# Attention with its query product ahead of the projections, a three-slot scan for the cell of a recurrence, and variance sums one tile later

## The reference, cut to what matters

```
q = (relu(x @ wq.T) + 1e-06) / softplus(scale);  k = (relu(x @ wk.T + pos) + 1e-06) / softplus(scale)
q, k = focus(q), focus(k)          # focus(t) = t^3 / |t^3| * |t|
z = 1 / (q . sum_j k_j + 1e-06)
y = (q @ (k^T v)) * z + depthwise_conv5x5(v)
out = y @ proj_w.T + proj_b
```

```
i = sigmoid(x U_i + h V_i + b_i); g = tanh(x U_c + h V_c + b_c); o = sigmoid(x U_o + h V_o + b_o)
cell = i * g + h * cell_before
h = o * tanh(cell)
```

## Time and profile before

| what | value |
|---|---|
| median of 3 runs | 1471.23 us (1469.86 to 1482.88) |
| profiled execution | 1470.42 us |
| its span, first to last instruction | 1468.5 us |
| instructions | 26362 |
| mean granted TensorE clock | 0.784 of full speed |

### The profile page before, as it was taken

The page is one execution under the profiler, slowest core; times in us unless marked ns, Lnnn a source line. Parts: engine busy times, 40 slices in busy tenths (PEclk is TensorE's granted clock), DMA queues, the critical chain, the costliest instruction groups (busy, mean ns, idle before and its releaser), DMA issues. The chain is left out here.

```text
span 1468.5 us, 26362 instructions
## 1 busy us (share of the span) xinstructions
PE 1125.3 (77%) x9003; PEld 648.5 (44%) x9003; DVE 888.7 (61%) x2711; ACT 505.0 (34%) x1330; POOL 245.2 (17%) x359
## 2 busy tenths in 40 slices
PE   6778877677998666666666656669947999999996
PEld 2356653343555344444444444437543333333332
DVE  6686736745776555555555555551264766666665
ACT  3443423452443222222222222234404334343432
POOL 3103102000000000000000000000001444454545
PEclk9899988878999855555555555569958999999999
DMA  7000000000000000000000000000005634554540
GB/s 270 0 2 2 1 2 0 1 0 1 1 0 1 1 1 0 0 0 0 0 0 0 0 0 0 0 1 0 0 0 108 136 95 112 103 111 105 105 111 7
DMA packets 23053, 46.90 MB, mean 32 GB/s; under 512 B 1616, under 2 KB 5840, under 8 KB 22608
## 3 DMA queue, kind: packets, MB, share of 16 engines
q1 hardware_dynamic: 22992, 46.10, 13.5%
HBM read 43.47 MB, written 2.62 MB: 31 GB/s over the span
## 5 line engine op out<-in xcount | busy, mean ns | idle before, releaser
L1587 PE MATMUL wide<-ls_h,ls_v 128*128 128x16 f16 x2304 | 104.8, 176 | 172.0 <-DVE ls_h L1680 172.0
L2017 PE MATMUL wide<-xpad,w 64*128 64x512 f32 x1024 | 228.7, 596 | 3.7 <-PEq L80 3.2
L2061 DVE TENSOR_TENSOR ex_hid<-wide,ex_gated 128x1024 f32<-128x1024 f32 x128 | 156.8, 1225 | 88.9 <-ACT ex_gated L2051 87.5
L2051 ACT ACTIVATE ex_gated<-wide 128x1024 f32<-128x1024 f32 x128 | 131.2, 1025 | 202.1 <-PE wide L2017 202.1
L1587 PEld LDWEIGHTS wide<-ls_h,ls_v 128*128 128x128 bf16 x2304 | 81.6, 106 | 241.0 <-DVE ls_h L1680 241.0
L1997 POOL TENSOR_TENSOR ex_acc<-ex_part,ex_acc 128x512 f32<-128x512 f32 x120 | 152.8, 1273 | 131.5 <-DVE ex_part L2072 117.0
L2017 PEld LDWEIGHTS wide<-xpad,w 64*128 64x128 f32 x1024 | 96.7, 187 | 134.5 <-issue 124.9
L1667 DVE SCALAR_TENSOR_TENSOR ls_ig<-ls_gates 128x16 f32<-128x16 f32 x256 | 53.0, 207 | 127.1 <-ACT ls_gates L1607 127.1
L1607 ACT ACTIVATE ls_gates<-wide 128x32 f32<-128x32 f32 x256 | 50.6, 198 | 229.0 <-PE wide L1592 229.0
L2029 PE MATMUL wide<-ex_hid,w 128*64 128x512 f32 x512 | 116.7, 598 | 0.0
L2072 DVE TENSOR_TENSOR ex_part<-wide,ex_d 128x1024 f32<-128x1024 f32 x64 | 78.4, 1225 | 30.1 <-PE wide L2029 27.3
(11 more groups left out here) (339 smaller groups left out, 1860.6 us busy)
## 6 DMA issues: line engine op xcount, KB each, us to landing
ex_d<-route SPq DMA_DIRECT2D x64, 512.0 KB, 7.8
par_attn<-in_attn SPq DMA_DIRECT2D x1, 2704.0 KB, 13.3
par_rest<-in_rest SPq DMA_DIRECT2D x1, 2139.0 KB, 17.8
L_xin<-in_x SPq DMA_DIRECT2D x8, 256.0 KB, 5.9
w<-in_w SPq DMA_DIRECT2D x1, 2048.0 KB, 22.2
out<-ex_acc SPq DMA_DIRECT2D x16, 128.0 KB, 4.4
w<-in_w SPq DMA_DIRECT2D x1, 512.0 KB, 23.0
route<-ro_dt SPq DMA_DIRECT2D x8, 64.0 KB, 1.7
```

The lines of the kernel that those rows point to most:

```text
L1587: pe.matmul(ig[:, g, :] if g < 2 else o, vp[part][:, g, :], h1[:], start=False, stop=False, skip_group_check=True)
L2017: mm = pe.matmul(pair_of_up(G, j)[:, h * TW:(h + 1) * TW], m.w12[r, (2 * e + w) * HID:(2 * e + w + 1) * HID], m.xn[r, t * TW:(t + 1) * TW] ...
L2051: act.activation(gated[:, n % 2, :], pair_of_up(n // GS, 2 * (n % GS))[:], ACT.Silu)\
L2061: dve.tensor_tensor(hid[:, n % (2 * GS), :], pair_of_up(n // GS, 2 * (n % GS) + 1)[:], gated[:, n % 2, :], ALU.mult).then_inc(s["hid_ready ...
```

## The change

In the attention the order of the full groups on TensorE becomes kv(G), attend(G), qkv(G+2), turn(G+1). On VectorE `divide(G)` stands ahead of `normalise(G+1)`, and the first sum is a step of its own. On ACT `turned(G)` stands ahead of `square_base(G+1)`. Mixed units are worked on with attend one unit behind, and k^T v of the mixed units alternates between wide[1] (banks 2 and 3) and wide[0] (banks 0 and 1). In the layer norm four centrings stand ahead of the first variance. In the recurrence the two instructions for the cell become one `tensor_tensor_scan` over 16 x 3 elements, in which the state is multiplied by `factors` and `addends` are added. The three slots of an image are (0, 1), (1, tanh of the input gate), (tanh g, hc), so the third result is g * (1 + t_i) + hc, which is twice the cell of before; the tanh behind it takes 0.5 times it. The gates, the cell and `hc` lie with a stride of three floats.

```diff
@@ attention, TensorE
-                pe.wait_ge(s["kvm_ready"], n)
+                pe.wait_ge(s["base_ready"], GROUPS if j % 2 else G + 1)
+                pe.wait_ge(s["kvm_ready"], n - 1 if n > FULL else n)
...
-            for G in range(GROUPS):
-                if G < FULL:
-                    kv(G)
+            for G in range(FULL):
+                if G % 4 == 0:
                     turn(G)
-                    if G + 2 < GROUPS:
-                        qkv(G + 2)
-                    attend(G)
+                kv(G)
+                attend(G)
+                qkv(G + 2)
+                if G % 4 == 3:
+                    finish_run(run_of(G))
                 else:
-                    for j in range(GU):
-                        kv_mixed(G, j)
-                        turn_mixed(G, j)
-                        attend_mixed(G, j)
-                if G in (3, 7, 9):
-                    finish_run(run_of(G))
+                    turn(G + 1)
+            for n in range(2 * GU + 1):
+                if n < 2 * GU:
+                    kv_mixed(FULL + n // GU, n % GU)
+                    turn_mixed(FULL + n // GU, n % GU)
+                if n:
+                    attend_mixed(FULL + (n - 1) // GU, (n - 1) % GU)
+            finish_run(2)
@@ attention, ScalarE
+            for G in range(FULL):
+                turned(G)
+                square_base(G + 1)
+                square_cube(G + 1)
+                root(G + 1)
+                values(G + 2)
+                if G + 1 == FULL:
                     masked(G + 1)
...
+            turned_mixed(FULL, 0)
+            square_base(FULL + 1)
+            turned_mixed(FULL, 1)
+            square_cube(FULL + 1)
+            turned_mixed(FULL, 2)
+            root(FULL + 1)
+            turned_mixed(FULL, 3)
+            masked(FULL + 1)
@@ attention, VectorE
+            for G in range(FULL):
+                base_of(G + 1)
+                mask(G)
+                cube_of(G + 1)
+                sum2(G + 1)
+                sum6(G + 1)
                 divide(G)
-                if G in (3, 7, 9):
+                normalise(G + 1)
+                if G % 4 == 3:
                     add_conv(run_of(G))
+            base_of(FULL + 1)
+            mask_mixed(FULL, 0)
+            cube_of(FULL + 1)
+            mask_mixed(FULL, 1)
+            sum2(FULL + 1)
+            mask_mixed(FULL, 2)
+            sum6(FULL + 1)
+            mask_mixed(FULL, 3)
+            normalise(FULL + 1)
+            divide(FULL)
+            for j in range(GU):
+                mask_mixed(FULL + 1, j)
+            divide(FULL + 1)
+            add_conv(2)
@@ layer norm, TensorE
-            for t in range(3):
+            for t in range(4):
                 centre(t)
-            for t in range(GT + 1):
+            for t in range(GT):
                 variance(t)
-                centre(t + 3)
-            variance(GT + 1)
+                centre(t + 4)
+            variance(GT)
             spread(0)
-            variance(GT + 2)
-            variance(GT + 3)
+            for t in range(GT + 1, TILES):
+                variance(t)
             spread(1)
@@ recurrence
+        N = HB * 3 + 2
+        flat = terms[:].rearrange("p z n -> p (z n)")
+        factors, addends = flat[:, 0:HB * 3], flat[:, N + 1:N + 1 + HB * 3]
+        cell, hc = cells[:, :, 2], addends.rearrange("p (b k) -> p b k", k=3)[:, :, 2]
+        two_gates = terms[:, :, 2:2 + HB * 3].rearrange("p z (b k) -> p z b k", k=3)[:, :, :, 0]
...
-                        act.activation(tc[:], cell[:], ACT.Tanh).then_inc(s["tc_ready"], 1)
+                        act.activation(tc[:], cell, ACT.Tanh, scale=0.5).then_inc(s["tc_ready"], 1)
...
-                        dve.scalar_tensor_tensor(ig[:], gates[:, 0, :], 1.0, gates[:, 1, :], ALU.add, ALU.mult)\
-                           .then_inc(s["ig_ready"], 1)
-                        dve.wait_ge(s["ig_ready"], t + 1)
                         dve.wait_ge(s["hc_ready"], t + 1)
-                        dve.scalar_tensor_tensor(cell[:], ig[:], 0.5, hc[:], ALU.mult, ALU.add)\
+                        dve.tensor_tensor_scan(cells[:].rearrange("p b k -> p (b k)"),
+                                               factors, addends, 0.0, ALU.mult, ALU.add)\
                            .then_inc(s["cell_ready"], 1)
```

79 lines of the change are left out of this document (26 added, 53 removed).

## The result

The changed kernel takes 1440.29 us (median of 4 runs, 1439.68 to 1441.81), the one before 1475.22 (median of 4, 1469.86 to 1482.88): a ratio of 0.9755 with a 95% interval of 0.9716 to 0.9795. The profiled execution took 1441.81 us, of which 1439.9 are its span; against the profiled one of before, 1470.42, that is 28.6 us less. By the ratio of all runs it is 36.0 us less (0.0245 x 1471.2). The two differ because the runs of before spread over 13 us and its profiled execution lies at their low end, while the profiled one of the changed kernel is the highest of its four.

The account below looks back on a forecast made before the run. No engine fills the span; the kernel is a row of stages, each with its own limit. Terms -33.0 + 4.0 + 0.2 - 8.8 - 0.2 = -37.8 us from 1470.4 give 1432.6, plus 0.8, rounded to 1434 us; range 1415 to 1448.

Parts of the forecast that it names:

- the likeliest case: Whole kernel: the forecast of 1434 us itself, own range 1426 to 1441 us, chance 0.62.
- The scan: Recurrence: two instructions become one scan at two cycles an element, 0.256 us, saving 0.129 us a step, 33.0 us.
- Both rate rivals: Recurrence scan: one element a cycle, 1422 us, chance 0.14; or as slow as the reciprocal, 1485 us, chance 0.04.
- Half of a bound of 7.9 us: Recurrence: the stride of three floats costs 0 to 7.9 us; half was taken, +4.0 us.
- PE's clock in the recurrence: Recurrence: clock taken to stay at 0.50; rival that it rises, 23 us less, 1411 us, chance 0.03.
- 2.5 + 3.5 = 6.0 us: Attention, mixed groups: masked copies start 2.5 us earlier; group 9, pipelined and nearer the low clock, gains 3.5 us.
- 2.8 us in all up to the mixed groups: Attention, full groups: gain from VectorE's filled hole and an earlier base(6), less later sums at run ends, 2.8 us.
- PE pays at the end of a run ... the sums start 0.6 us later: Attention, run ends: qkv waits for mask and attend, so the convolution sums start 0.6 us later against base.
- costs some 0.4 us in a group in which the clock is low: Attention, full groups: kv's cover is base alone, 1.13 against 0.76 us of matmul; low clock costs some 0.4 us.
- base(6) was to come 2.0 us earlier: Attention, group 6: with divide done before, base(6) is limited by qkv(6) and moves from 140.9 to 138.9.
- the attention gives nothing, since PE's clock falls at other places: Rival on the attention: kv and qkv then come late, no gain there, 1443 us, chance 0.11.
- The layer norms: Four layer norms: order changes, not the sum; 0 for three, 0.2 us gained before the recurrence, bounds ±0.3 each.

Follow-up runs that it names:

- the long scan: Changed kernel with the scan run over 96 elements instead of 48, the 48 more being zeros nobody reads: 1467.04 us, ratio 0.9943.
- the kernel with the strides alone: Kernel before with gates, cell and hc at a stride of three floats, without the scan: 1482.37 us, ratio 1.0053.
- the half alone: Kernel before with only the two mixed groups of the attention reordered, the eight full groups as before: 1464.10 us, ratio 0.9927.
- the kernel with the old full groups: Changed kernel with its eight full attention groups put back to the order of before on all three engines: 1440.31 us, ratio 0.9778.

## Why the prediction was right in sum, and where it was not

**The total.** 1434 us were forecast and 1440.29 measured, inside the range of 1415 to 1448 and, barely, inside the likeliest case's own of 1426 to 1441. As a ratio the forecast was 1434 / 1471.23 = 0.9747, and 0.9755 was measured. An agreement that close is luck. Between the two profiled executions 37.8 us less were forecast and 28.6 were measured; the attention gave 5.7 us less than forecast, the recurrence 2.2 less, and stages that nobody edited took 2.0 us more. The ratio came near all the same because the other executions of before were slower than its profiled one: the sum had 0.8 us for that, and the median of the four is 4.8 us above it.

**The scan, right.** 0.256 us forecast, 0.258 measured; 0.035 to ACT's start, 0.04 measured. The argument (the result of an element must be there before the next one starts, so two cycles each) chose the right rate, and the long scan shows the slope itself: 2.08 ns where 2.04 were taken. The runs show the rate and not its reason. The Trainium skill (DVE: opcode table, instruction layouts, handler registers and perf-mode slots, section 6, Datapath and trigger behaviour) says that the built-in scan runs at half throughput; the trace agrees, with 2.08 against 1.02 ns an element. Both rate rivals fall, 1.02 and 6.2 ns.

**The strides, undersized.** Half of a bound of 7.9 us was taken, 4.0; the two ACT instructions cost 23 ns a step, 5.9 us. Scan, starts and strides together: 1.740 us less the 0.105 gained is the 1.63 seen, 26.8 us for the recurrence against 33.0 - 4.0 = 29.0 forecast. Of the 2.2 us missing 1.9 are the strides. The measured 5.9 lie midway between the half that was taken and the whole bound; the kernel with the strides alone, in which VectorE writes a strided cell as well, shows 7.7. The Trainium skill (SBUF — State Buffer, section SBUF: two separate sides) says that each access that crosses to a new 16-byte line pays a penalty, without a figure for it; the trace agrees that there is one at a step of 12 bytes, 15 ns for 32 elements. What scaled wrong was the interpolation: the price was assumed to fall with the length of the step, from 64 bytes in the earlier trace rows down to 12, and per element it hardly does (0.64 ns there; 15 ns for 32 elements and 8 for 16 here, 0.5 ns each).

**PE's clock in the recurrence, right.** It stayed at the lower level; PE's fillers did not delay the nine matmuls, which waited for `h` as before (0.28 us in the step shown, 141.6 of 144.9 us over the stage).

**The mixed groups, right in kind and size.** 2.5 + 3.5 = 6.0 us were forecast for groups 8 and 9; the marks show 2.7 and 4.2 (15.12 to 12.45 and 16.55 to 12.33 us), and the half alone 7.1. Group 9 was nearer the full clock than assumed: only its first unit was slow after the idle time. The masked copies start 9.2 us after the first kv of group 8 instead of 11.86 and so come earlier within the group, as worked out; their place near 186 was missed (192.18), since they were to gain 2.8 us from the full groups and lost 3.9 there.

**The full groups, wrong sign.** This is the step that failed: "2.8 us in all up to the mixed groups". 3.95 us were lost instead, an error of 6.8 us: 3.0 at the two runs' ends, 1.7 behind the second run, 1.2 at base(6) and 1.0 in group 1. (For groups 5 to 7 the forecast has 0.75 us without its working; two periods at 0.42 would be 0.84.) Its parts:

- The period without the hole, 8.29 us, came as forecast wherever the clock was full, and `divide` of group 4 lost its wait of 4.46 us.
- "PE pays at the end of a run ... the sums start 0.6 us later" costed the swapped order only at the full clock. The run's end took 2.10 us more, not 0.6, with the clock at 0.54 in the projections; the transposes just behind it ran at 0.53. The kernel with that order put back at the run's end alone has 14.22 us there, at the clock 1.00, and is 7.4 us faster in the stage. That this order at this place is what starts the loss in the changed kernel is shown by it.
- "costs some 0.4 us in a group in which the clock is low": such a group was there (group 2), and it cost a `base` wait of 0.98 us on qkv, not a mask wait on kv. The thinner cover that mattered was that of the projections, which start behind `attend`; the prediction looked only at kv's.
- base(6) was to come 2.0 us earlier since qkv(6) would start at the same time. It starts 3.5 us later (136.40 against 132.92): 2.1 us come from the run's end and most of the rest from the slow transposes behind it, which stand ahead of the output projection and so of GpSimd's gather. It runs at a low clock too, and base(6) still waits 1.06 us for it. The same slow transposes stand behind the second run, and no term had the 1.7 us that the first mask of group 8 comes later for it.

The rival "the attention gives nothing, since PE's clock falls at other places" named this mechanism and gave it 0.11. It was right for half the stage. Its "against", that the hole is filled whatever the clock does, is true and not enough: the hole is filled and a wait for qkv opens in its stead.

**The layer norms, right.** Forecast -0.2 us in all, and alone they make no difference in the time. By the traces three of the four give 0.16, 0.43 and 0.16 us, one of them beyond its bound of 0.3.

**What no term had.** Code that nobody edited moved by +2.0 us in all between the two traces: whitening -2.1, slice attention +1.6, experts +2.5. The experts' first 70 us, before and after:

```profile
1111.00:1181.00 70.00, 66.23 (x302) 26.38 (x302) 43.09 (x36) 30.06 (x32) 24.19 (x19) 1.00 0.65 133
```
```profile
1080.00:1150.00 70.00, 66.14 (x289) 26.01 (x290) 41.65 (x34) 28.39 (x31) 22.27 (x18) 0.95 0.62 129
```

The clock fell in a piece of it in one and not in the other, and 13 matmuls fewer were done in the same time. Such stages also move between two executions of one program: in the changed kernel and in the same kernel once more the whitening takes 48.18 and 50.19 us, the slice attention 135.33 and 133.64, the sigmoid attention 65.88 and 67.90, where the attention takes 152.21 and 152.23.

**Still open.** Why the clock falls in exactly these stretches. Shown is that it follows holes of PE at the runs' ends (filling them, and making one of them shorter, removed it from there) and that one order can have it in different places in two kernels. What decides between the two is not shown; the start of the stage (72.1 against 74.1 us) went with it in the kernel with the old full groups, but the new attention took nearly the same from 72.4 and from 74.1.

## What to carry to other kernels

Before two instructions that depend on each other are replaced by a scan, price it over all slots, spacers included (here 158 ns and 2.08 ns a slot, twice the time an element of an ordinary instruction), and add what the spacers do to every neighbour that reads or writes with a step: here the scan gained 26.8 us net, after the strides had taken 5.9 back. Where an engine's clock depends on its own holes, "who waits for whom" at the full clock is half of an answer: for each moved instruction ask which holes of PE it makes longer, and try the move per place, not per loop (the order of two of eight groups put back gave 7.4 us in the stage, and that of all eight put back gave nothing). And compare more than one execution of before: its profiled one alone would have put this change at 28.6 us instead of 36.

## What the runs showed of the hardware that was not expected

- The scan of VectorE takes 158 ns + 2.08 ns an element (48: 258 ns, 96: 358 ns).
- ACT pays for a small step too: 32 elements written 12 bytes apart 213 instead of 198 ns, 16 read so 223 instead of 215; VectorE writing 16 so 182 instead of 175.
- A scan that overlaps a GpSimd instruction takes about 0.25 us more, whatever its length: 496 to 511 instead of 258 ns over 48 elements, 594 to 619 instead of 358 over 96. The two-input instruction in its place took about 0.26 us more (440 instead of 175).
- The same attention code took 148.2 us in one kernel and 154.9 in another, with the granted clock 0.90 and 0.86; two other forms of it were steady within 0.7 us over four kernels each.
